# Attention with a routed feed-forward on one core: gate logits as columns of V's projection, routing moved to the last batch, raw weights split in place, SP's transfers reordered

## What is computed

```python
Q, K, V = (einsum('bse,hec->bhsc', xn, W) + b for W, b in ...)   # 16 heads, Q and K 128 wide, V 64
A1, A2 = Q1 @ K1.T / 8, Q2 @ K2.T / 8                            # the halves of Q and K
P = softmax(A1) - lam * softmax(A2);  O = P @ V
attention = layernorm(concat(O) @ Wo + bo) * gamma + beta, times 0.2
logits = t @ switch_w + switch_b;  e = argmax(logits)            # t: 4096 rows, 8 experts
ffn = (gelu(t @ w1[e] + b1[e]) @ w2[e] + b2[e]) * max(softmax(logits))
```

## Time and profile before

| what | us |
|---|---|
| runs, median (lowest to highest) | 1940.58 (1940.29 to 1941.86) |
| profiled execution, its own time | 1935.32 |
| its span | 1933.5 |
| TensorE busy | 1856.4 (96%) |
| VectorE, ScalarE, GpSimd busy | 1512.5, 1417.2, 703.8 |
| first scores of pair 0 | 65.60 |
| first transfer of the feed-forward stage | 1513.26 |

### The profile page before, as it was taken

One profiled execution on the slowest core, in us unless ns is written; L12 is line 12 of the kernel. 1 busy time (PEld: TensorE's weight loads), 2 busy tenths in 40 slices (PEclk: granted clock), 3 DMA queues, 4 the chain that ended last, 5 costly groups with the idle time before them and its releaser, 6 DMA issues. The chain is left out here.

```text
span 1933.5 us, 33239 instructions
## 1 busy us (share of the span) xinstructions
PE 1856.4 (96%) x10753; PEld 1442.1 (75%) x10753; DVE 1512.5 (78%) x2500; ACT 1417.2 (73%) x3298; POOL 703.8 (36%) x757
## 2 busy tenths in 40 slices
PE   5999999999999999999999999999999499999997
PEld 4866777777777777777777777777776399999896
DVE  5588888888888888888888888888888376666265
ACT  5588888888888888888888888888888376666100
POOL 2144333333333333333322333322223375555443
PEclk9799999999999999999999999999999799999999
DMA  8689888888888888888898888888885666666898
GB/s 290 181 219 258 212 221 224 225 223 234 225 222 225 225 228 228 207 231 227 220 232 230 225 222 227 222 228 227 220 212 137 241 208 238 234 236 212 285 385 285
DMA packets 228132, 446.09 MB, mean 231 GB/s; under 512 B 28962, under 2 KB 119888, under 8 KB 221968
## 3 DMA queue, kind: packets, MB, share of 16 engines
q1 hardware_dynamic: 223216, 434.02, 81.5%
q0 software_dynamic: 4768, 10.25, 1.8%
HBM read 184.34 MB, written 58.50 MB: 126 GB/s over the span
## 5 line engine op out<-in xcount | busy, mean ns | idle before, releaser
L536 ACT ACTIVATE e<-p_score,nmax 128x512 f32<-128x512 f32 x1024 | 695.4, 685 | 149.1 <-DVE nmax L743 145.5
L743 DVE TENSOR_REDUCE nmax<-p_score 128x2 f32<-128x1024 f32 x512 | 621.8, 1214 | 209.2 <-PE p_score L850 205.3
L386 POOL TENSOR_SCALAR e<-e,rrec,lam 128x512 f32<-128x512 f32 x512 | 394.6, 771 | 971.0 <-DVE rrec L708 971.0
L850 PE MATMUL p_score<-ks,qs 128*128 128x512 f32 x2048 | 580.3, 405 | 3.4 <-ACT e L536 3.3
L850 PEld LDWEIGHTS p_score<-ks,qs 128*128 128x128 f32 x2048 | 366.2, 189 | 177.6 <-issue 101.7
L815 PE MATMUL p_proj<-xh,w 128*128 128x512 f32 x1024 | 386.6, 418 | 5.8 <-POOL xl L370 3.7
L715 DVE SCALAR_TENSOR_TENSOR pm<-e,rrec 128x512 f32<-128x512 f32 x512 | 385.3, 753 | 0.7 <-POOL e L386 0.7
L470 ACT COPY pT<-p_tr 128x512 f32<-128x512 f32 x512 | 301.1, 588 | 96.8 <-PE p_tr L860 89.1
L860 PEld LDWEIGHTS p_tr<-consts,pm 128*128 128x128 f32 x2048 | 248.9, 140 | 88.5 <-issue 27.4
L860 PE MATMUL p_tr<-consts,pm 128*128 128x128 f32 x2048 | 308.5, 273 | 4.3 <-ACT pT L470 4.3
L875 PE MATMUL p_pv<-pT,v 128*64 128x512 f32 x1024 | 247.7, 605 | 2.0 <-DVE oT L720 2.0
(11 more groups left out here) (141 smaller groups left out, 1895.8 us busy)
## 6 DMA issues: line engine op xcount, KB each, us to landing
ks<-k_parts SPq DMA_DIRECT2D x512, 256.0 KB, 4.4
qs<-q_parts SPq DMA_DIRECT2D x512, 128.0 KB, 2.7
w<-weight_parts_scratch SPq DMA_DIRECT2D x56, 1024.0 KB, 9.3
w<-in_w SPq DMA_DIRECT2D x46, 1024.0 KB, 7.2
oT_scratch<-oT SPq DMA_DIRECT2D x64, 512.0 KB
op<-oT_scratch SPq DMA_DIRECT2D x32, 1024.0 KB
wv<-weight_parts_scratch SPq DMA_DIRECT2D x56, 256.0 KB, 7.9
weight_parts_scratch<-w SPq DMA_DIRECT2D x8, 1024.0 KB
```

The lines of the kernel that those rows point to most:

```text
L386: nc.gpsimd.tensor_scalar(e2, e2, rrec[:, g % 4, 1:2], lam[:, 0:1], ALU.mult, ALU.mult).then_inc(s_e2, 1)
L536: nc.scalar.activation(ex[:, g % EX, m, :], p_score[g % 2][:, m, :], ACT.Exp, bias=nmax[:, g % 2, m:m + 1], accum_out=rsum[:, g % 4, m:m + ...
L743: vec.tensor_reduce(nmax[:, g % 2, :], p_score[g % 2][:, :, :], AXX, ALU.max, negate=True).then_inc(s_max, 1)
L850: last_op = nc.tensor.matmul(p_score[g % 2][:, m, :], qs[j][u][:, m, qt * P:(qt + 1) * P], ks[j][u][:, m, part, :], start=(part == 0), sto ...
```

## The change

- The gate's weights are eight more columns beside V's weights (264 instead of 256 columns) for the first two V projections of each batch; the second half goes to the bank of p_pv, and VectorE adds the gate's bias to eight columns, V's bias to the rest. The logits' matmuls in the front are gone.
- Routing runs one operation a step from step 452 (pair 56, batch eight), the ranks at step 462, the exponential at 454, the scatters one a step from 480.
- Raw weights are loaded to the place of their own low part, high parts are copied from there and the low part is subtracted in place. So they are prepared two pairs ahead instead of three, in other steps: on ScalarE at 0, 2, 3, 4, on GpSimd at 1, 4, 6. V's raw weights are a transfer of their own.
- Fillers: projections at steps 0, 2, 4, 6, V's at 3, the products with V at 5 and at step 1 of the pair after. V's projections run one pair ahead; the first two no longer come at steps 4 and 5 but at 1 and 3. One oT instead of two.
- Front: the first root, normalisations and transposes come ahead of the weights' split; statistics are taken ahead of the second half of the moments' steps; VectorE normalises groups 7 to 15.
- SP: in the loop q0's and k0's copies are first, then the load of w and the store of oT, then q1's, the store of split weights, k1's, and raw weights last. In the front raw weights of pair 2 and the store of pair 1's come behind all stores of xn.

```diff
-ACT_GROUPS = 13
+ACT_GROUPS, DVE_GROUPS = tuple(range(7)), tuple(range(7, 16))
 EX = 3
-FIRST_V = 4
-ROUTE_OPS = (2, 1, 3, 3, 0, 0, 0, 3, 3, 3, 2, 2, 2, 1)
+WVC = 2 * P + NE
+ROUTE_FROM = 452
+ROUTE_OPS = (1,) * 8 + (0, 0, 2) + (1,) * 14
+SCATTER_FROM = 480
...
-        w = [sb(f"w{j}", [P, 2, WQK], F32R) for j in range(2)]
-        wv = [sb(f"wv{a}", [P, 2, KT, 2, P], F32R) for a in range(2)]
+        w_raw, w = then([(f"w_raw{j}", [P, 2, WQK], F32) for j in range(2)],
+                        [(f"w{j}", [P, 2, WQK], F32R) for j in range(2)])
+        wv_raw, wv = then([(f"wv_raw{a}", [P, 2, KT, WVC], F32) for a in range(2)],
+                          [(f"wv{a}", [P, 2, KT, WVC], F32R) for a in range(2)])
...
-        SHIFTED, ONEHOT = 3, 9
-        RANK_STEP = 6
+        SHIFTED, ONEHOT = 2, 8
+        EXP_STEP, RANK_STEP, ONES_STEP = ROUTE_FROM + 2, ROUTE_FROM + 10, ROUTE_FROM - TPP
+        RANK_PAIR = RANK_STEP // TPP
 
         ORDER = ("q0", "k0", "q1", "k1")
-        AT_STEP = {0: "q0", 1: "k0", 2: "q1", 3: "k1"}
-        V_STEP = 6
-        PV_STEP = {5: (0, 1), 7: (2, 3)}
+        AT_STEP = {0: "q0", 2: "k0", 4: "q1", 6: "k1"}
+        V_STEP = 3
+        PV_FIRST, PV_LAST = 5, 1
+
+        def bank_of(pair, what):
+
+            return p_proj[(5 * pair + ("q0", "k0", "v", "q1", "k1").index(what)) % 2]
...
+        def v_banks(n):
+
+            own = bank_of(n, "v")
+            if n == 0:
+                return [(p_tr[:, :, :].rearrange("p k s -> p (k s)"), 0), (p_pv[:, :], 0)]
+            return [(own[:, :], 0), (p_pv[:, :], 0)] if with_logits(n) else [(own[:, :], 0), (own[:, :], 2 * P)]
...
             def load_raw(pair):
-                sp.dma_start(raw_of(pair)[:, :], ins["w_attn"][pair]).then_inc(s_raw[pair if pair < 3 else 0], 16)
+                j = pair % 2
+                if pair >= 2:
+                    sp.wait_ge(s_proj, 4 * (pair - 2) + 4)
+                    sp.wait_ge(s_wst[j], 32 * (pair // 2))
+                sp.dma_start(w_raw[j][:, 1, :], ins["w_attn"][pair, :, 0:WQK]).then_inc(s_raw[j], 16)
+
+            def load_raw_v(pair):
+                if pair >= 4:
+                    sp.wait_ge(s_vp, 2 * (pair // 2 - 2) + 2)
+                    sp.wait_ge(s_wst[pair % 2], 32 * ((pair - 4) // 2 + 1))
+                sp.dma_start(wv_of(pair, 1, wv_raw),
+                             ins["w_attn"][pair, :, WQK:WPAIR].rearrange("p (k d) -> p k d", d=P)
+                             ).then_inc(s_rawv[pair % 2], 16)
...
+            load_raw_v(0)
+            for n in range(2, 9):
                 load_x(n)
             sp.dma_start(sw[:, :, :], ins["sw"]).then_inc(s_sw, 16)
             sp.dma_start(bias[:, :, :], ins["attn_bias"]).then_inc(s_bias, 16)
             sp.dma_start(lam[:, :], ins["lam"]).then_inc(s_bias, 16)
             sp.dma_start(swb[:, :], ins["swb"]).then_inc(s_bias, 16)
-            for n in range(5, 9):
-                load_x(n)
-            load_raw(1)
             for n in range(9, GROUPS):
                 load_x(n)
-            load_raw(2)
+            load_raw_v(1)
+            load_raw(1)
             sp.dma_start(bv[:, :], ins["bv"]).then_inc(s_bias, 16)
             for n in range(2):
                 store_xn(n)
             sp.wait_ge(s_zero, 1)
             sp.dma_start(token_d.rearrange("(p n) a -> p (n a)", p=P), no_token[:, :]).then_inc(s_zeroed, 16)
             store_w(0)
-            for n in range(2, 4):
+            for pair in (2, 3):
+                load_raw_v(pair)
+            for n in range(2, 5):
                 store_xn(n)
             for what in "qk":
                 spread(0, what, 0)
-            load_raw(3)
-            for n in range(4, 9):
+            for n in range(5, 11):
                 store_xn(n)
-            store_w(1)
             for what in "qk":
                 spread(1, what, 0)
-            for n in range(9, GROUPS):
+            for n in range(11, GROUPS):
                 store_xn(n)
-            store_w(2)
+            load_raw(2)
+            store_w(1)
 
             for pair in range(NPAIRS):
-                if pair + 2 < PAIRS and pair >= 1:
-                    store_w(pair + 2)
-                    if pair + 3 < PAIRS:
-                        load_raw(pair + 3)
+                if pair + 1 < NPAIRS:
+                    for what in "qk":
+                        spread(0, what, pair + 1)
                 if PAIRS <= pair + 2 < NPAIRS:
-                    if pair + 2 < PAIRS + 2:
-                        for p in range(PAIRS):
-                            sp.wait_ge(s_wst[p % 2], 32 * (p // 2 + 1))
                     load_w(pair + 2)
+                if pair >= 2:
+                    store_o(pair - 2)
                 if pair % 2 == 0 and QT <= pair // 2 + 2 < ITERS:
                     load_wv(pair // 2 + 2)
                 if pair + 1 < NPAIRS:
-                    for u in range(2):
-                        for what in "qk":
-                            spread(u, what, pair + 1)
-                if pair >= 2:
-                    store_o(pair - 2)
+                    spread(1, "q", pair + 1)
+                if pair + 4 < PAIRS:
+                    load_raw_v(pair + 4)
+                if pair + 2 < PAIRS:
+                    store_w(pair + 2)
+                if pair + 1 < NPAIRS:
+                    spread(1, "k", pair + 1)
+                if pair + 3 < PAIRS:
+                    load_raw(pair + 3)
             store_o(NPAIRS - 2)
...
+                if pair + 2 < PAIRS:
+                    if st == 1:
+                        low_v(pair + 2)
                     if st == 4:
-                        low_qk(pair + 3, 0)
-                    if st == 5:
-                        low_qk(pair + 3, 1)
+                        low_qk(pair + 2, 0)
+                    if st == 6:
+                        low_qk(pair + 2, 1)
...
+                if 0 <= g - SCATTER_FROM < NT:
+                    c = g - SCATTER_FROM
...
                 act.wait_ge(s_pv, pair + 1)
-                if pair == 0:
-                    act.wait_ge(s_route, 1)
-                if pair >= 2:
-                    act.wait_ge(s_ost[pair % 2], 16 * (pair // 2))
-                nc.scalar.copy(oT[pair % 2][:, 0, :], p_pv[:, :]).then_inc(s_ohi, 1)
-
+                if pair >= 1:
+                    act.wait_ge(s_ost, 16 * pair)
+                nc.scalar.copy(oT[:, 0, :], p_pv[:, :]).then_inc(s_ohi, 1)
...
+            root(0)
+            normalise(0)
+            normalise(1)
             scale_q(0)
             high_qk(0, 0)
             evacuate(0)
             evacuate(1)
+            act.wait_ge(s_xT, 2)
             nc.scalar.copy(xh[0][:, :, :], xT[:, :, 0:S]).then_inc(s_xhi, 1)
+            high_qk(0, 1)
+            high_v(0)
+            act.wait_ge(s_sw, 16)
+            nc.scalar.copy(wv[0][:, 0, :, 2 * P:WVC], sw[:, :, :]).then_inc(s_swhi, 1)
...
+            root(2)
             scale_q(1)
             high_qk(1, 0)
             high_qk(1, 1)
+            high_v(1)
+            evacuate(7)
             evacuate(8)
+            high_part(0, "q1")
+            evacuate(9)
+            evacuate(10)
+            high_part(0, "k1")
+            for n in range(11, GROUPS):
+                evacuate(n)
...
+                    if st == 0:
+                        high_v(pair + 2)
                     if st == 2:
-                        scale_q(pair + 3)
+                        scale_q(pair + 2)
                     if st == 3:
-                        high_qk(pair + 3, 0)
+                        high_qk(pair + 2, 0)
                     if st == 4:
-                        high_qk(pair + 3, 1)
+                        high_qk(pair + 2, 1)
...
+            statistics(0)
             shift_and_scale(0)
+            statistics(1)
             shift_and_scale(1)
+            normalise(7)
+            normalise(8)
...
+            statistics(2)
             dve.wait_ge(s_bq, 1)
             dve.wait_ge(s_lam, 1)
             low_part(0, "q0")
             low_part(0, "k0")
             shift_and_scale(2)
-            for n in range(ACT_GROUPS, GROUPS):
+            for n in range(9, GROUPS):
...
+                if g == 2:
+                    add_bv(0)
+                if st == V_STEP + 1 and pair + 1 < NPAIRS:
+                    add_bv(pair + 1)
+                if st == 2 and pair >= 2:
                     low_o(pair - 2)
-                for _ in range(ROUTE_OPS[g] if g < len(ROUTE_OPS) else 0):
+                for _ in range(ROUTE_OPS[g - ROUTE_FROM] if 0 <= g - ROUTE_FROM < len(ROUTE_OPS) else 0):
...
+            project(0, "q0")
+            project(0, "k0")
             for n in range(2, 9):
                 transpose_x(n)
-                if n >= 3:
-                    logits(n - 1)
-                if n == 4:
-                    project(0, "q1")
-                if n == 5:
-                    project(0, "k1")
-            logits(8)
-            for n in range(9, GROUPS):
+            project(0, "q1")
```

(75 more changed lines are left out.)

297 lines of the change are left out of this document (125 added, 172 removed).

## The result

The changed kernel takes 2066.4 us (median of 4 runs, 2060.3 to 2073.3) where the kernel before took 1940.7: a ratio of 1.065, 95% interval 1.061 to 1.068. It is slower by 126 us; 1920.8 had been predicted. The profiled execution has a span of 2064.5 against 1933.5, +131.0.

A forecast was written before the change was run, and what follows sets the result against it. TensorE was taken as the bound, busy throughout the steady loop, with the DMA engines a hidden second. From 1940.6 us, -29 (front) + 8 (pairs 1 to 5) - 2 (steady) + 2 (routing) + 1.2 (end) gave 1920.8; range 1903 to 1946.

The forecast's parts named there:

- the steady pairs: Pairs 6 to 55: same 22.17 us a pair, -2 in all (bounds -8 and +3), load of w landing in 6.7, hidden.
- rival (a): Steady pairs: load of w lands late, a pair takes 14.2 + L from L = 8.0 on; 1943 to 1994 us; chance 0.18.
- The estimate from the Trainium skill: Load of w: 6.15 us for 1 MB by itself behind 1.5 of queue, so L of 7.7.
- Pairs 1 to 5: Batch 0: each raw load waits in a chain of 25.7 us a period; 127.1 against 119.1, +8 (bounds -8 and +17).
- The front: Up to pair 1's first scores: earlier projections, then waiting for pair 2's w_raw until some 53.4; -29 us (bounds -22 and -36).
- at worst 3 us, covered by the wait for w_raw: Front: port lock slowing VectorE's normalisations while GpSimd splits pair 1's weights, at worst 3 us, hidden.
- The order of steps: Pairs 6 to 55: same operations in another order, half of the even pairs' 0.15 us saved over 25 pairs, -2.
- Routing: Pairs 56 to 59: some 9 us of VectorE operations, one a step, mostly fitting; +2 us (bounds 0 and +9).
- The scatters: Issued one a step: 2.15 us of GpSimd's time in a mean step of 2.77, so hidden.
- Rival (d): Scatters: port lock makes each 1 us longer, GpSimd's step 3.15 against 2.77, 12 us in all, 1933; chance 0.04.
- (b): Batch 0: raw weights come in time, pairs 1 to 5 take 111 us, -16 on the forecast, 1905; chance 0.17.
- (c): Front: DMA engines full, scores start early but wait for copies, pair 6 starts about as before; 1936 to 1943; chance 0.08.

The follow-up runs named there:

- Run 3: Changed kernel, store of oT and V's weights moved behind q1's copies, SyncE waiting until k0's copies landed before issuing the load of w: 2125.7 us.
- run 4: Kernel before, with only the load of w moved from the head of the pair's list behind k0's copies: 1941.1 us, ratio 0.9995.
- run 5: Changed kernel, in batch 0 the raw q and k load issued ahead of k1's copies and the store of split weights behind them: 2015.2 us.
- Run 9: Changed kernel with the edits of run 1 and run 5, plus pair 2's raw load earlier and pair 1's weight store later in the front: 1908.4 us.
- run 1: Changed kernel with the load of w moved back to the head of SyncE's list for the pair: 1954.3 us, ratio 1.007 to the kernel before.
- mended in four places: Changed kernel with the edits of run 1, run 5 and Run 9, and GpSimd splitting V's weights at step 0: 1903.5 us, ratio 0.980.

## Why the prediction was wrong

**The step that failed** is the last of the steady pairs: "1.5 of queue, 4.2 for its own 1 MB at 237 to 264 GB/s, 1 for the landing, 6.7. Hidden, with 1.4 to spare." Measured: 9.9. Run 3 has 7.0 for the load with nothing ahead, where the second and third term gave 5.2; the copies ahead cost 2.3, not 1.5; the requests behind, which rival (a) named, cost 0.6 and stood at nothing. Two of the terms had little under them: half of 1 MB at the same 237 to 264 GB/s is 2.0 to 2.2 and not 1.5, and no row or run shows the 1 for the landing by itself. The load was also taken to be issued 15.4 into the pair; it came at 16.9, because a first wait delays the next load. The row that measured this very load stood in the earlier trace rows at 8.6 to 12.4, and I argued it away because more had been issued ahead of it there. In run 4, with k0's copies alone right ahead, it was no shorter but 10.5. Rival (a) had the mechanism, the threshold (L = 8.0) and the price a pair: at 9.9 its formula gives 24.1, measured 23.98. It should have been the forecast; its chance of 0.18 was the second mistake, since every landing on record (8.6 and more) was above its threshold.

**The estimate from the Trainium skill** (DMA: Bandwidth & Descriptors, section "Bandwidth": 6.15 us for 1 MB by itself) was 7.7 for L, nearer than my 6.7 and still 2.2 short. The page has the figure for a transfer that GpSimd issues; SyncE issues this one. The run with the copies landed first, 7.0, comes within 0.9 of it.

**Pairs 1 to 5** had the right chain in the right order, and every pair showed ScalarE's wait for w_raw. Two terms of it were too small. From the landing to the end of the low half 14.7 were counted; it is 136.63 - 118.61 = 18.0, and in it ScalarE stands twice for TensorE's transposes (1.06 and 1.16), the first of them right behind TensorE's stretch at the 1.2 GHz level. From there to the next landing 11 were counted, measured 12.4. 30.4 in the place of 25.7 a period. That the raw load waits at SyncE behind a store which waits for GpSimd was written down and priced as traffic; run 5 shows that it was order: 39 us come back with the same bytes.

**The front** came as told: first projection at 15.54 (15.5), first scores at 39.7 (37), the wait for w_raw(2) in the place foreseen. It lasted until 58.4, not 53.4, and that is nearly all of the 5.6 by which the gain fell short. Run 9 gives it back: from 30.4 in the changed kernel to 24.0.

```profile
58.42 0.63 ACT L466 ACTIVATE w_raw<-w_raw 128x512 f32<-128x512 f32 x1 [10.12 <-DMA w_raw<-in_w_attn]
```

The first scores came 2.7 late, and on the way to them stands a delay that the prediction named. VectorE's normalisation of half a group (L630, 18 in all) takes 0.40 in the median, but the three that began while GpSimd split pair 1's weights took 0.82, 1.35 and 1.36, each of them ending just behind a split:

```profile
30.58 2.56 POOL L407 TENSOR_TENSOR w<-w_raw,w 128x512 fp32r<-128x512 f32 x2 [13.03 <-ACT w L472]
33.10 0.78 POOL L401 TENSOR_TENSOR wv<-wv_raw,wv 128x256 fp32r<-128x256 f32 x1
```

```profile
L630 DVE TENSOR_SCALAR xin<-xin,mom x3: 818/1354/1362, 30.7 to 33.2; 128x256 f32<-128x256 f32 x3
```

These are 2.3 us beyond three of 0.40, inside the "at worst 3 us, covered by the wait for w_raw", and they were covered: ScalarE waited until 58.4 all the same. No run takes them away, so how much of the 2.7 they are stays open.

**The order of steps** was right where nothing waits: run 1 has pairs 6 to 55 at 1109.7 against 1112.8, -3.1 (-2). **Routing** too: pairs 56 to 59 take 91.1 in run 1 against 88.7, +2.4 (+2).

**The scatters** "hidden" were priced on GpSimd alone. There they fit: L452 shows issues of 1.07 to 1.21 as before. They cost on the DMA engines, 15.8 of the 23; of the other 7.2, 1.1 is V's projection in pair 62 and the rest the late load of w. Rival (d), the port lock at the scatters, fell with the same row. The Trainium skill's rule of an exclusive lock (SBUF — State Buffer, section "SBUF: two separate sides") so shows nothing on the scatters' issues; the trace agrees with it in the front, by the three normalisations above.

```profile
L452 POOL DMA_INDIRECT token_scratch<-consts,slot_u x32: 1067/1067/1212, 1528.7 to 1632.0; - x32
```

**The other rivals.** (b), raw weights in time, fell in every pair's wait. (c), full DMA engines that take back the front's gain: the gain was gone, pair 6 started at 223.9 where it had started at 212.5, but by the order on SyncE, with the DMA engines at 0.69 in pairs 1 to 5. The range's upper end, 1946, cut off two thirds of (a). The time fell beyond even its 1994, because three stretches went over together: 87, 35 and 23.

## What to carry to other kernels

When a change moves a load later in an in-order queue, take the longest landing of that load that the trace has, not one built from bandwidth, and compare it with the room left; add the delay of every step that the change also shifts, since here the place in the list (run 4) and the later projection of k0 (run 1) were each free and together cost 1.9 us in each of the 48 steady pairs. Put loads that depend on nothing recent at the head of an in-order list, and behind them what waits for fresh results. A change whose parts lie in different stretches should be measured by stretch: this one, mended in four places, is 2% faster than the kernel before (ratio 0.980) and not 6.5% slower.
